# Products of the unit matrix in three waits of TensorE

## What is computed

```python
x = _layernorm(x + L0_attn(x))            # linear attention, 8 heads
x = _layernorm(x + L0_xattn(x, ctx))      # cross attention, 16 heads
x = _layernorm(x + L0_ffn(x))             # gate, up and down products with quantized activations
x = _layernorm(x + L1_attn(x))            # causal scores of a metric, no softmax
x = _layernorm(x + L1_xattn(x, ctx))      # normalized queries and keys, a null key, layer norm
x = _layernorm(x + L1_ffn(x))             # a real 256x256 map made by two Fourier products, plus bias
```

## Time and profile before

| | |
|---|---|
| runs | 1424.16, 1425.21, 1429.18 us |
| median | 1425.21 us |
| profiled execution | 1429.01 us, of which its span 1427.2 us |
| mean granted clock of PE | 0.95 |
| PE busy | 1249.9 us, 88% of the span |
| DVE busy | 1042.0 us, 73% |
| ACT, POOL busy | 516.8 us, 36%, and 263.7 us, 18% |

### The profile page before, as it was taken

How to read it: one execution, slowest core, us unless ns; L and a number is a source line. 1 busy time by engine, 2 the same in 40 slices (tenths; PEclk the granted TensorE clock), 3 DMA queues, 4 the chain that set the end, 5 groups by cost and what they waited for, 6 DMA issues and landing times.

```text
span 1427.2 us, 18392 instructions
## 1 busy us (share of the span) xinstructions
PE 1249.9 (88%) x7324; PEld 832.9 (58%) x7324; DVE 1042.0 (73%) x1930; ACT 516.8 (36%) x605; POOL 263.7 (18%) x184
## 2 busy tenths in 40 slices
PE   7899999979899999722778999999999999998964
PEld 4465666656544544311555676867768686766553
DVE  3579889986345598996343687978878797968684
ACT  1334434434434567674011333332323323341320
POOL 0011111110000000043100321414142231414140
PEclk9999999999999999856889999999999999999998
DMA  5001000004651246495221110121111100000000
GB/s 211 15 16 31 30 31 30 16 15 126 210 199 59 74 167 216 154 391 178 86 96 54 44 52 31 33 73 37 59 54 52 39 15 28 26 24 23 1 15 15
DMA packets 47781, 107.86 MB, mean 76 GB/s; under 512 B 10704, under 2 KB 31312, under 8 KB 44240
## 3 DMA queue, kind: packets, MB, share of 16 engines
q1 hardware_dynamic: 43536, 104.59, 21.0%
q10 hardware_dynamic: 4160, 2.10, 0.5%
HBM read 62.64 MB, written 44.04 MB: 75 GB/s over the span
## 4 chain that ended last, share of the span: by engine, by line
PE 74%; DVE 15%; ACT 4%; issue 3%; DMA 2%; POOL 1%; SPq 0%; POOLq 0%; DVEq 0%; ACTq 0%
PE ps L1290 8%; PE ps L1350 7%; PE ps L1177 6%; PE ps L1025 6%; PE ps L1076 6%; PE ps L779 3%; PE ps L1323 3%; PE ps L1237 3%; PE ps L927 2%; PE ps L1261 2%; PE ps L852 2%; PE ps L1272 2%; PE ps L1367 2%; PE ps L870 2%; PE ps L1337 2%
## 5 line engine op out<-in xcount | busy, mean ns | idle before, releaser
L1350 PE MATMUL ps<-arena 128*128 128x256 f32 x512 | 120.0, 388 | 6.7 <-ACT arena L1775 6.7
L1290 PE MATMUL ps<-arena 128*128 128x512 f32 x256 | 117.6, 598 | 0.0
L1350 PEld LDWEIGHTS ps<-arena 128*128 128x128 f32 x512 | 98.5, 195 | 28.0 <-ACT arena L1775 10.2
L1802 POOL TENSOR_TENSOR arena<-arena 128x4 f32<-128x4 f32 x48 | 49.4, 1033 | 340.7 <-DVE arena L1957 340.7
L2283 DVE TENSOR_TENSOR arena<-ps,arena 128x2048 f32<-128x2048 f32 x32 | 73.3, 2291 | 41.5 <-PE ps L1237 41.0
L1863 POOL TENSOR_TENSOR arena<-arena 128x16 f32<-128x16 f32 x32 | 91.9, 2908 | 34.1 <-DVE arena L2312 34.1
L1177 PE MATMUL ps<-arena 128*128 128x256 f32 x384 | 89.3, 392 | 9.0 <-DVE arena L2236 6.7
L1177 PEld LDWEIGHTS ps<-arena 128*128 128x128 f32 x384 | 74.7, 197 | 20.2 <-issue 7.1
L1025 PE MATMUL ps<-arena 128*128 128x512 f32 x192 | 85.5, 602 | 1.2 <-ACT arena L1502 1.2
L1076 PE MATMUL ps<-arena 128*128 128x512 f32 x192 | 84.7, 595 | 0.0
L1290 PEld LDWEIGHTS ps<-arena 128*128 128x128 f32 x256 | 46.3, 190 | 48.2 <-issue 44.5
(11 more groups left out here) (262 smaller groups left out, 2621.8 us busy)
## 6 DMA issues: line engine op xcount, KB each, us to landing
v_scratch<-arena SPq DMA_DIRECT2D x7, 1536.0 KB, 12.7
arena<-v_scratch SPq DMA_DIRECT2D x7, 1536.0 KB, 6.8
up_scratch<-arena SPq DMA_DIRECT2D x6, 1536.0 KB, 7.3
arena<-up_scratch SPq DMA_DIRECT2D x6, 1536.0 KB, 10.2
vw_scratch<-arena SPq DMA_DIRECT2D x32, 256.0 KB, 3.9
arena<-x_scratch SPq DMA_DIRECT2D x16, 512.0 KB, 4.4
arena<-vw_scratch SPq DMA_DIRECT2D x8, 1024.0 KB
arena<-x SPq DMA_DIRECT2D x8, 512.0 KB, 5.3
```

The lines of the kernel that those rows point to most:

```text
L1290: last = mm(flat(p % 2), w["cos_wq"][:, k, p * P:(p + 1) * P], xt4[:, k], start=k == 0, stop=k == NC - 1)
L1350: last = mm(flat(2)[:, C:2 * C], cos_pt[:, p], cos_vw[:, par, p], start=p == 0, stop=p == NP - 1)
L1802: g.tensor_tensor(var[0], var[1], neghalf[:, 0:NT], ALU.pow)\
```

## The change

`keep_busy(n)` issues n matmuls of 128x512. The stationary operand is the unit matrix `ident`, the moving one the first 512 columns of `cos_wq`, the target bank 7. Nothing reads the result, and no semaphore is raised. The first call stands between the two waits ahead of loop two, the second ahead of the wait of `dn_turn` in batch 0, the third ahead of the wait of `cos_turn_x` in batch 7.

```diff
             pe.wait_ge(ev("vw_copied"), 2 * NP)
+            def keep_busy(n):
+                for i in range(n):
+                    mm(flat(7), ident, w["cos_wq"][:, 0, 0:4 * P], start=True, stop=True)
+
+            keep_busy(6)
             pe.wait_ge(ev("scale_ready"), QUANTIZED["v"])
...
             def dn_turn(b, par):
+                if b.first():
+                    keep_busy(4)
                 wait(pe, "y3_ready", b)
                 wait_previous(pe, "met_masked", b, 4)
                 turn_rows(5, y3[:, par], "dn_turned")
...
             def cos_turn_x(b, par):
+                if b.last():
+                    keep_busy(8)
                 wait(pe, "y5_ready", b)
                 wait(pe, "cos_pt_copied", b, NT, NT)
                 wait_ahead(pe, "met_masked", b, 2, 2, 4)
                 turn_rows(3, y5, "cos_x_turned")
```

## The result

The changed kernel takes 1419.94 us in the median of 8 runs (1417.51 to 1421.90), the kernel before 1425.29 us in the median of 8 (1422.90 to 1429.18). The ratio is 0.9959, with a 95% interval from 0.9944 to 0.9973: 0.4% faster, which is 5.8 us by the ratio and 5.35 by the medians. The forecast was 1419.0.

What follows compares the result with a forecast made beforehand. It took PE, on the chain and at a low granted clock behind three waits, to bound the kernel. Gains of 2.1 + 1.1 + 3.0 = 6.2 us take the median 1425.2 to 1419.0 us; range 1415.5 to 1424.0.

Steps and rivals of the forecast that it cites:

- The cost of a product: Each added matmul is two PE passes, 0.43 us each at the high clock, 0.83 at the low; other engines lose nothing.
- Place 1: Wait ahead of loop two: twelve passes raise the clock before the first down projection; gain 2.1 us, bounds 0.3 to 2.3.
- Place 2: First turn of loop two: eight passes, 2.5 us stay idle, clock falls later and for shorter; gain 1.1 us, bounds -3.8 to 2.5.
- with 3.4 us low: First turn of loop two: low-clock stretch of 3.4 us against 6.8 before, so the loss is 1.2 to 1.5 instead of 2.5.
- The rival of the late fall: First turn of loop two: clock falls as L1191 starts, losing 3.8 us there; total gain 1.3, 1423.9 us; chance 0.14.
- Behind place 2: Further waits after loop two's first turn, where the clock can fall or not: no change taken, 1.5 us allowed either way.
- Place 3: Last turn: sixteen passes keep the clock high through the turn and last projection; gain 3.0 us, bounds 0 to 3.1.
- the 1.2 us which stay idle are harmless: Last turn: some 1.2 us stay idle, as long as earlier waits behind which both groups ran at full speed.
- The slower rival: Clock stays at 0.50, added passes outlast the waits ahead of loop two and the last turn; 3.2 us lost, 1428.4; chance 0.04.
- the products do nothing for the clock: Rival: the clock does not count unit-matrix products as work; no gain, 0 to 1 us lost, 1425.5 us; chance 0.04.
- its sentence on the Trainium skill's page: Ahead of loop two, if transposes do not count for the clock: passes end 678.6 to 679.2, gain 1.3 instead of 2.1.

Runs made afterwards that it cites:

- p1_only: Kernel before plus only the six products ahead of loop two; 1422.92 us, ratio 0.9978 to the kernel before.
- p2_only: Kernel before plus only the four products behind the first down projection; 1425.88 us, ratio 1.0001 to the kernel before.
- back_all: Kernel before with PE's waits of over 1 us in the last two turns filled with products, nothing earlier; 1419.78 us, ratio 0.9950.
- p3_only: Kernel before plus only the eight products ahead of the last turn; 1426.05 us, ratio 1.0002 to the kernel before.
- p1_ten: Kernel before plus ten products, instead of six, ahead of loop two and no others; 1426.14 us, ratio 0.9999 to the kernel before.

## Why the prediction was right

The forecast was a gain of 6.2 us to 1419.0; it is 5.35 by medians, at 1419.94, inside the range, and less than 0.5%, as forecast. By its steps:

- **The cost of a product** (two passes, 0.43 us each at the high clock and 0.83 at the low one): right. Twelve passes took 7.01 us across the rise, eight 3.60, sixteen 7.03. That they cost the other engines nothing, as assumed, also fits: the waits from PE's last work of its own to its next are 6.72, 6.01 and 8.07 us with the products in them, against 6.74, 6.01 and 8.06.
- **Place 1**, forecast 2.1 us: right in each link, the rise 5.15 us after the start of work (4.5 to 6.1 foreseen), an overrun of 0.1 us or less, 10.60 us for the down projection. p1_only measured 3.1 (1.3 to 5.0). What was not foreseen is what the clock does behind it: in p1_only's trace M is 1.5 us less and the last stretch 1.8 more.
- **Place 2**, forecast 1.1 us: not borne out. The runs of p2_only give 0, though their interval just reaches the 1.1 us, and in the changed kernel's trace the place gains nothing. The step that failed is "with 3.4 us low", which took the shortest low stretch of the trace for this one; in the changed kernel it was 6.84 us, as before. In p2_only it was 3.4, and the gain of 0.7 us there was lost again behind it. The fall does come later, as forecast, in the turn and not in the wait. The rival of the late fall described what is seen in kind, L1173 partly fast and L1198 slower, but it priced it at -3.8. Turn and met_project took 0.3 more than in the kernel before (and 0.3 less than in p1_only), since L1207 and the down projection behind it were at full speed again.
- **Behind place 2** I took no change and allowed 1.5 us either way; the trace has 1.5 us less in M. p1_only has the same M, and back_all, with nothing at either place, an M of 53.36 and an F of 31.32. So M falls with the instants of the clock, and its 1.5 us is not the work of place 2. Further on the third down projection took 1.7 us less and the last stretch 1.8 more, and these happen to cancel.
- **Place 3**, forecast 3.0 us: mis-sized. It is 3.0 in one sort of execution and 0.6 in the other, 1.3 between the two profiled ones. The sentence that failed is that the 1.2 us which stay idle are harmless because the clock held through waits as long. The rows it rested on were read rightly, and the pattern there is nearly the same, two waits of 1.11 us around a turn of 1.09 (L1200). But waits of this length go both ways, as p3_only's trace and the changed kernel's show, and the forecast took one of the two for certain. What decides between them stays open.
- **The slower rival** (the added work becomes the wait) was not met at the sizes chosen; p1_ten shows its price, 3.3 us for four products too many. That the products do nothing for the clock is excluded by p1_only.

So the total was right partly by luck. In the two profiled executions the 4.7 us are made up of 2.3 at the first down projection, -0.3 at place 2, 1.5 in M, 1.7 at the third down projection, -1.8 in the last stretch ahead of the tail, and 1.3 in the tail. Of the forecast's terms of 2.1, 1.1 and 3.0 the first is there, the second is not and the third by less than half, 3.3 us together, and what lies behind place 2, which was put at nothing, adds 1.4. It is the mechanism and place 1 that were foreseen; the other two terms were not.

A small slip of the prediction changes nothing: by its own rates the twelve passes of its sentence on the Trainium skill's page would end by 679.3, not 679.2.

What stays open: why 11 runs of p3_only had no gain, where by the traces they should have had 0.6 to 3.0 us. The interval allows a gain of 1.6 us, so 0.6 is not excluded and 3.0 is. If most of its runs were of the second sort, that would be the 0.6; the runs give a time and a mean clock, no place in the program, and so cannot show it. They do show that its four slowest runs (1427.8 to 1428.6) have the lowest mean clock, 0.946 to 0.947, and its four fastest (1422.8 to 1423.4) 0.951. The starts of loop two scatter by more than the effect, and one trace for each kernel cannot tell how often each sort occurs. No experiment for that was made.

## What to carry to other kernels

Where PE waits a few microseconds for another engine and its next work lies on the chain, products of no use can hold or regain its high clock, and in these traces a product that nothing reads, in a free bank, cost the other engines nothing that the length of the waits shows. But the rests that stay can give it back: 2.6 us with 1.2 behind it did in both traces, two of 1.1 and 1.2 around a short group did in one of two, and filling the short waits around the pipeline's ends too gained more (0.9886) than the three long waits (0.9959). Size each filling from the wait's own row and from the clock at which PE comes to it: a product too many costs its full time, and one that runs fast where it was counted slow leaves a rest.

## What the runs showed of the hardware that I had not expected

- Transposes held the clock as products did, in one trace each: with 56 of them in the wait it fell 10.6 us behind the last cos_out, with sixteen passes of products 10.65, with nothing 3.8.
- In these traces the clock's falls do not come at arbitrary distances from the work. In ten of them, with different work ahead of loop two and in its first turns, the last fall before the tail came either 28.9 or 13.3 us ahead of the last cos_out's end, to 0.1 us, and the tail has two lengths accordingly. A profile of one execution shows one of them.
- The same instructions with the same waits around them, 1.2 and 1.1 us, kept the clock in one trace (p3_only) and lost it in another (the changed kernel). So did a wait of 2.98 us, kept in the kernel before and lost in the changed one, at a place that the change does not touch.
